# Order of the small products, weights for twelve expert pairs ahead, and when the other pairs' weights are asked for, in a five-stage transformer kernel

## The reference

```
x = x + attention(norm(x))          # 16 heads of 16, rotary embedding, softmax over 512 keys
x = x + moe(norm(x))                # 64 experts, 8 per token, 128 rows at most per expert
x = x + forget_attention(norm(x))   # linear attention with a decay per head and step, biases
x = x + moe(norm(x))                # same weights as the first
```

```
probs = softmax(x @ router_w.T); topk_w, topk_ids = top_k(probs, 8); topk_w /= sum(topk_w)
# each expert e takes its first 128 rows:
h = silu(xb @ w_gate[e]) * (xb @ w_up[e])      # 256 -> 192
y = h @ w_down[e]                              # 192 -> 256, scaled by topk_w, added to its rows
out = sum over the 8 experts of a token + silu(x @ sg) * (x @ su) @ ws_down   # shared expert
```

## Time and profile before

| | us |
|---|---|
| median of 3 runs | 2755.16 (2754.28 to 2756.10) |
| the profiled execution, its time | 2756.48 |
| its span, first to last instruction | 2754.8 |
| attention_project, 0 to 258 | 258 |
| attention_mix, 258 to 1152 | 894 |
| moe_front, moe_experts (first) | 260, 273 |
| forget_attention, 1685 to 2222 | 537 |
| moe_front, moe_experts (second) | 257, 276 |

### The profile page before, as it was taken

How to read it: one execution, slowest core, us unless ns; L and a number is a source line. 1 busy time by engine, 2 the same in 40 slices (tenths; PEclk the granted TensorE clock), 3 DMA queues, 4 the chain that set the end, 5 groups by cost and what they waited for, 6 DMA issues and landing times. The chain is left out here.

```text
span 2754.8 us, 47087 instructions
## 1 busy us (share of the span) xinstructions
PE 2424.5 (88%) x14506; PEld 1327.5 (48%) x14506; DVE 1737.0 (63%) x3661; ACT 1272.0 (46%) x2564; POOL 1128.4 (41%) x1350
## 2 busy tenths in 40 slices
PE   8996899999999999699878883899999979888885
PEld 5653233323333333366456662566666556556663
DVE  7996887788778877288422222688888669632221
ACT  3452576676666667444223220545545424322221
POOL 6888000100000010133136663677777723226664
PEclk9997799999999999899989995999999989999997
DMA  5554323232232321255439982011111036537985
GB/s 165 189 190 160 103 91 95 83 92 84 89 92 88 97 81 47 72 164 195 146 102 247 233 194 54 16 36 36 36 38 30 21 120 202 177 101 193 236 224 104
DMA packets 289374, 325.30 MB, mean 118 GB/s; under 512 B 28944, under 2 KB 270752, under 8 KB 289184
## 3 DMA queue, kind: packets, MB, share of 16 engines
q1 hardware_dynamic: 257536, 274.49, 32.4%
q0 software_dynamic: 27136, 46.16, 8.3%
q10 hardware_dynamic: 4512, 2.40, 0.3%
HBM read 217.23 MB, written 105.19 MB: 117 GB/s over the span
## 5 line engine op out<-in xcount | busy, mean ns | idle before, releaser
L672 DVE TENSOR_REDUCE a_row_max<-a_ps_m 128x2 f32<-128x1024 f32 x512 | 615.0, 1220 | 126.5 <-PE a_ps_m L570 124.4
L720 ACT ACTIVATE a_probs<-a_ps_s 128x512 f32<-128x512 f32 x1024 | 545.7, 600 | 293.7 <-PE a_ps_s L596 293.4
L596 PE MATMUL a_ps_s<-a_qs,a_ks 98*128 98x512 bf16 (+1 forms) x1024 | 319.1, 390 | 9.8 <-ACT a_probs L720 7.5
L611 PE MATMUL a_ps_o<-a_probs,a_va 128*32 128x512 f32 x2048 | 272.3, 604 | 0.8 <-ACT a_o_sb L729 0.8
L1511 POOL TENSOR_TENSOR b_spread<-b_decay,held_own_sb 128x512 f32<-128x512 f32 x256 | 269.1, 1084 | 8.6 <-DVE b_weight L1609 8.6
L570 PE MATMUL a_ps_m<-a_ks,a_qs 48*128 48x512 bf16 x1024 | 207.1, 401 | 45.6 <-DVE a_row_max L672 40.0
L570 PEld LDWEIGHTS a_ps_m<-a_ks,a_qs 48*128 48x128 bf16 x1024 | 49.3, 93 | 342.0 <-DVE a_row_max L672 169.4
L545 POOL DMA_DIRECT2D x<-a_xo x32 | 23.5, 735 | 442.6 <-DVE a_xo L705 442.6
L1609 DVE TENSOR_TENSOR b_weight<-b_ps_s,b_spread 128x512 f32<-128x512 f32 x256 | 163.6, 681 | 17.9 <-PE b_ps_s L1744 17.9
L596 PEld LDWEIGHTS a_ps_s<-a_qs,a_ks 98*128 98x128 bf16 (+1 forms) x1024 | 69.8, 97 | 157.5 <-ACT a_probs L720 86.2
L516 POOL CAST a_high<-a_row_max 128x32 bf16<-128x32 f32 x32 | 6.7, 209 | 321.2 <-DVE a_row_max L672 321.2
(11 more groups left out here) (326 smaller groups left out, 5097.5 us busy)
## 6 DMA issues: line engine op xcount, KB each, us to landing
parts<-a_parts SPq DMA_DIRECT2D x16, 1536.0 KB, 6.2
a_qs<-parts SPq DMA_DIRECT2D x384, 64.0 KB, 2.2
a_ks<-parts SPq DMA_DIRECT2D x384, 64.0 KB, 2.2
m_w_gu<-in_L_ffn_w_gate_dram SPq DMA_DIRECT2D x64, 384.0 KB, 4.0
m_w_gu<-in_L_ffn_w_up_dram SPq DMA_DIRECT2D x64, 384.0 KB, 5.4
m_w_d<-in_L_ffn_w_down_dram SPq DMA_DIRECT2D x64, 384.0 KB, 6.7
rows<-m1f_row SPq DMA_DIRECT2D x16, 640.0 KB, 3.1
rows<-m2f_row SPq DMA_DIRECT2D x16, 640.0 KB, 3.1
```

What stands on the lines that cost most here:

```text
L596: nc.tensor.matmul(s_bank(name, step)[:], ks[u][0:K_ALL[e], h, t * P:(t + 1) * P], qs[u][0:K_ALL[e], h, :], start=True, stop=True).then_in ...
L611: last = nc.tensor.matmul(ps_o[VW * j:VW * (j + 1), :], va[n.u][:, t, (h0 + j) * VW:(h0 + j + 1) * VW], probs[:, group % 2, j, t, :], star ...
L672: nc.vector.tensor_reduce(row_max[:, n.k // 4 % 2, t, :, n.p % 4], m_bank(name, step)[:], AX.X, ALU.max).then_inc(m_drained, 1)
L720: nc.scalar.activation(probs[:, group % 2, j, t, :], s_bank(name, step)[:], ACT.Exp, scale=DK ** -0.5).then_inc(s_drained, 1)
```

## The change

- **attention_mix:** in the lists of PE and DVE and in M_ORDER, the turn of the output moves to behind the second score product, ahead of the values' product; the turn of the maxima to behind it. Both stood between the second and the third of the products for row maxima, and now stand between the first and the second.
- **Expert weights:** there are twelve buffers. Four are memory of their own, four ("early") are the memory that the routing part of `moe_front` uses for x, row and the gates, and four ("kept") that of x_turned. `moe_front` loads twelve pairs: four at steps 16 to 19, four at steps 20 to 23 after the routing part has ended, and four at steps 19, 21, 24 and 26 after the last shared round that lies in their memory. It waits for all twelve at its end. `kept_at` lays the rounds in x_turned so that this works.
- **moe_experts:** the remaining 20 pairs' weights wait for y0 as before, and for a new semaphore `landed`, which POOL raises when its wait for the scatter before has ended. Pair i (12 to 31) waits for the count i - 12 + (i - 12) * 7 // 20 + 1, so 20 requests are spread over 26 scatters. DVE does `compare` and `set_aside` first in a step.
- **forget_attention:** `project_features` is split in `first_features` and `last_features`, with `sum_logs` and `turn_att` between them; ACT does `decays` before `copy_att`.

```diff
@@ -331,7 +332,7 @@
         return at
 
     M_RING, S_RING = 2, 3
-    M_ORDER = [("max0", 0, 1, 0), ("max1", 0, 1, 0), ("shift", L_TURN, 4, 3), ("output", L_OTURN, 2, 1), ("max2", 0, 1, 0), ("max3", 0, 1, 0),
+    M_ORDER = [("max0", 0, 1, 0), ("output", L_OTURN, 2, 1), ("shift", L_TURN, 4, 3), ("max1", 0, 1, 0), ("max2", 0, 1, 0), ("max3", 0, 1, 0),
                ("out0", L_OUT[0], PAIRS, PAIRS - 1), ("out1", L_OUT[1], PAIRS, PAIRS - 1)]
     S_ORDER = [(f"score{i}", L_S, 1, 0) for i in range(8)] + [(f"att{q}", L_ATT[q], PAIRS, PAIRS - 1) for q in range(2)]
     M_AT, S_AT = turns_in_order(M_ORDER, TOTAL + 16), turns_in_order(S_ORDER, TOTAL + 16)
@@ -651,9 +652,8 @@
                     last.then_inc(m_filled, 1)
                 return stage
 
-            walk_pairs(pe, [(0, max_products(0)), (L_S, scores(0)), (L_S, scores(1)), (L_MIX + 1, mix_values(1)),
-                            (0, max_products(1)), (L_S, scores(2)), (L_S, scores(3)), (L_TURN, turn_shift), (L_OTURN, turn_output),
-                            (0, max_products(2)), (L_S, scores(4)), (L_S, scores(5)), (L_MIX, mix_values(0)),
+            walk_pairs(pe, [(0, max_products(0)), (L_S, scores(0)), (L_S, scores(1)), (L_OTURN, turn_output), (L_MIX + 1, mix_values(1)),
+                            (L_TURN, turn_shift), (0, max_products(1)), (L_S, scores(2)), (L_S, scores(3)), (0, max_products(2)), (L_S, scores(4)), (L_S, scores(5)), (L_MIX, mix_values(0)),
                             (0, max_products(3)), (L_S, scores(6)), (L_S, scores(7)),
                             (L_ATT[0], turn_att(0)), (L_ATT[1], turn_att(1)), (L_OUT[0], project(0)), (L_OUT[1], project(1))])
 
@@ -705,7 +705,7 @@
                     nc.vector.tensor_tensor(xo[:, q], out, xr[n.u][:, 2 * q:2 * q + 2, :], ALU.add).then_inc(m_drained, 1)
                 return stage
 
-            walk_pairs(dve, [(0, maxima(0)), (0, maxima(1)), (L_TURN, copy_shift), (L_OTURN, normalise), (0, maxima(2)), (0, maxima(3)),
+            walk_pairs(dve, [(0, maxima(0)), (L_OTURN, normalise), (L_TURN, copy_shift), (0, maxima(1)), (0, maxima(2)), (0, maxima(3)),
                              (L_OUT[0], residual(0)), (L_OUT[1], residual(1))], unrolled=2)
 
...
@@ -871,13 +885,28 @@
                 for to, source in pair_of_weights(const, i, i):
                     sp.dma_start(to, source).then_inc(w_loaded, 16)
 
-            in_turn([(lambda i: i, lambda i: load(i + XB - 1), ROUNDS - XB + 1), (lambda i: ROUNDS + 2 * i, load_weights, HELD),
+            def load_early(i):
+                if i == 0:
+                    sp.wait_ge(gate_done, ROUNDS)
+                    sp.wait_ge(x_was_turned, 2 * ROUNDS)
+                    for k in range(RB):
+                        sp.wait_ge(row_stored[k], 16 * ROUNDS // RB)
+                load_weights(OWN + i)
+
+            def last_round(i):
+
+                return 6 + -(-(i + 1) * XT // KEPT_BUFFERS) - 1
+
+            def load_kept(i):
+                sp.wait_ge(gated, 3 * (last_round(i) + 1))
+                load_weights(OWN + EARLY_BUFFERS + i)
+
+            in_turn([(lambda i: i, lambda i: load(i + XB - 1), ROUNDS - XB + 1), (lambda i: ROUNDS + i, load_weights, OWN),
+                     (lambda i: ROUNDS + L_GATE + 1 + i, load_early, EARLY_BUFFERS), (lambda i: shared_at(last_round(i)) + 1, load_kept, KEPT_BUFFERS),
                      (shared_at, load_residual, ROUNDS),
                      (lambda i: i + L_GATE, store_rows, ROUNDS), (lambda r: shared_at(r) + 1, store, ROUNDS)])
             sp.wait_ge(pad_stored, 16)
-            sp.wait_ge(w_loaded, 48 * HELD)
-            for k in range(RB):
-                sp.wait_ge(row_stored[k], 16 * ROUNDS // RB)
+            sp.wait_ge(w_loaded, 48 * (OWN + EARLY_BUFFERS + KEPT_BUFFERS))
             for k in range(2):
                 sp.wait_ge(stored[k], 16 * ROUNDS // 2)
 
@@ -1022,8 +1051,7 @@
                 def stage(s):
                     act.wait_ge(x_was_turned, 2 * s + q + 1)
                     wait(act, gated, 3 * (s - XT + 1))
-                    first = (TPR * (s % XT) + 2 * q) * P
-                    nc.scalar.activation(x_turned[:, :, first:first + 2 * P], ps_x[:], ACT.Copy).then_inc(x_kept, 1)
+                    nc.scalar.activation(x_turned[:, kept_at(s), :, 2 * q * P:2 * (q + 1) * P], ps_x[:], ACT.Copy).then_inc(x_kept, 1)
                 return stage
 
...
     PAIRS, C = E // 2, 2
     FH = F // C
-    WB, XB, YB, DB = 4, 8, 4, 6
-    LEAD = 2
+    WB, XB, YB, DB = len(const["w_buffers"]), 8, 4, 6
     slots, slots_f = const["slots"], const["slots_f"]
 
...
@@ -1218,7 +1245,7 @@
             for i in range(WB, PAIRS):
                 k = i % WB
                 sp.wait_ge(y0_ready, i - WB + 1)
-                sp.wait_ge(x_turned, i - LEAD + 1)
+                sp.wait_ge(landed, i - WB + (i - WB) * 7 // (PAIRS - WB) + 1)
                 for to, source in pair_of_weights(const, i, k):
                     sp.dma_start(to, source).then_inc(w_loaded[k], 16)
 
@@ -1236,6 +1263,7 @@
                 pool.wait_ge(y1_done, i + 1)
                 pool.wait_ge(y0_done, i + 1)
                 wait(pool, scattered, 32 * i)
+                passed_by(pool, landed)
 
                 for j, index in ((1, slots_1[:, i:i + 1]), (0, slots[:, 2 * i:2 * i + 1])):
...
@@ -1352,7 +1380,7 @@
                 wait(dve, scattered, 32 * (i - YB + 1))
                 nc.vector.tensor_copy(y[:, i % YB, 0, :], ps_y[i % 2][:, 0, :]).then_inc(y0_done, 1)
 
-            in_turn([(L_GU, hidden(0)), (L_DOWN, copy_first), (L_GU, hidden(1)), (L_SAME, compare), (L_SAME, set_aside)])
+            in_turn([(L_SAME, compare), (L_SAME, set_aside), (L_GU, hidden(0)), (L_DOWN, copy_first), (L_GU, hidden(1))])
 
 
 def forget_attention(nc, x_in, x_out, const):
@@ -1683,8 +1711,8 @@
                 wait(act, out_ready, n - 1)
                 nc.scalar.activation(attT[:, n % 2], ps_w[:, 0:2, :], ACT.Copy).then_inc(attT_done, 1)
 
-            in_turn([(L_VF, evacuate_values), (L_PV, copy_output), (L_TURN, evacuate_x), (L_LOGS, gate_exponentials), (L_OUT, copy_att),
-                     (L_UPTO, decays), (L_FEED, exponentials)])
+            in_turn([(L_VF, evacuate_values), (L_PV, copy_output), (L_TURN, evacuate_x), (L_LOGS, gate_exponentials), (L_UPTO, decays),
+                     (L_OUT, copy_att), (L_FEED, exponentials)])
 
         @block.tensor
         def _(pe):
@@ -1726,13 +1754,15 @@
                 wait(pe, decay_done, n)
                 nc.tensor.matmul(ps_a[:, 0:D], later[:], log_upto[:, n % 2].rearrange("p h t -> p (h t)"), start=True, stop=True).then_inc(sums_ready, 1)
 
-            def project_features(n):
+            def first_features(n):
                 sg, blk = n // SG, n % SG
                 pe.wait_ge(xnT_done, SG * (sg + 1))
                 wait(pe, phi_done, n)
-                for c in range(2):
-                    last = nc.tensor.matmul(ps_p[:], w_qk[:, c, blk * P:(blk + 1) * P], xnT[:, sg % 2, c, :], start=c == 0, stop=c == 1)
-                last.then_inc(p_ready, 1)
+                nc.tensor.matmul(ps_p[:], w_qk[:, 0, blk * P:(blk + 1) * P], xnT[:, sg % 2, 0, :], start=True, stop=False)
+
+            def last_features(n):
+                sg, blk = n // SG, n % SG
+                nc.tensor.matmul(ps_p[:], w_qk[:, 1, blk * P:(blk + 1) * P], xnT[:, sg % 2, 1, :], start=False, stop=True).then_inc(p_ready, 1)
 
             def scores(n):
                 sg, g = n // SG, n % SG
@@ -1775,8 +1805,8 @@
                     last = nc.tensor.matmul(out, attT[:, n % 2, c, :], w_o[:, c, :], start=False, stop=c == 1)
                 last.then_inc(out_ready, 1)
 
-            in_turn([(L_VF, project_values), (L_S, scores), (L_PV, mix_values), (L_TURN, turn_x), (L_OUT, turn_output), (L_FEED, project_features),
-                     (L_OUT, turn_att), (L_UPTO, sum_logs), (L_OUT, project_out)])
+            in_turn([(L_VF, project_values), (L_S, scores), (L_PV, mix_values), (L_TURN, turn_x), (L_OUT, turn_output), (L_FEED, first_features),
+                     (L_UPTO, sum_logs), (L_OUT, turn_att), (L_FEED, last_features), (L_OUT, project_out)])
 
 
...
@@ -1846,8 +1878,17 @@
 
     def mixture(tag, x_in, x_out):
         with (nc.sbuf_tensor(tag + "_slots", [P, E], u32) as slots, nc.sbuf_tensor(tag + "_slots_f", [P, E], fp32) as slots_f,
-              nc.sbuf_tensor(tag + "_w_gu", [P, PAIRS_HELD, 2, 2, 2, F], fp32) as w_gu, nc.sbuf_tensor(tag + "_w_d", [F // 2, PAIRS_HELD, 2, 2, D], fp32) as w_d):
-            const = dict(held, slots=slots, slots_f=slots_f, w_gu=w_gu, w_d=w_d, w_gate=a["L0_ffn_w_gate"], w_up=a["L0_ffn_w_up"], w_down=a["L0_ffn_w_down"])
+              nc.sbuf_tensor(tag + "_own", [P, OWN * (GU + WD)], fp32) as own, nc.sbuf_tensor(tag + "_early", [P, EARLY * (GU + WD)], fp32) as early,
+              nc.sbuf_tensor(tag + "_kept", [P, KEPT * (GU + WD)], fp32) as kept):
+
+
+            buffers = []
```

(6 more changed lines are left out.)

53 lines of the change are left out of this document (33 added, 20 removed).

## The result

| | before | after |
|---|---|---|
| median, us | 2754.72 | 2707.82 |
| range of the runs, us | 2751.31 to 2756.10 | 2707.73 to 2711.89 |
| span of the profiled execution, us | 2754.8 | 2705.8 |

The ratio of the two is 0.9839, 95% interval 0.9823 to 0.9855: some 44 us are gained (47 by the medians), where 85 were forecast. The time lies in the range for 8 in 10 (2638 to 2712), near its upper end, and outside the forecast's own range of 2650 to 2695.

The account below looks back on a forecast made before the run. Expert stages were taken as bound by a scatter chain stretched by weight transfers, the two attention stages by PE. From 2756.48 us, -42 - 30 - 13 + 0 = -85 gave 2671.5, median 2670; own range 2650 to 2695, 8 in 10 2638 to 2712.

Parts of the forecast that it names:

- rival 3: attention_mix and forget_attention: the PE edits only move their waits, DVE holding the next product or step; 2714 us, chance 0.08.
- the period of a loaded scatter: Expert stages: distance between pairs' first scatters with a weight request, taken as 7.4 us; 219 against 238.6, -20 per stage.
- rival 1: Expert stages: a request at the scatter's start doubles its transfers, 6.5 + 2.35 = 8.85 us per loaded period; 2729, chance 0.14.
- The ceiling of 9.62 to 10.12: Expert stages: upper limit in us for a loaded period, from profiled distances with a request just behind the scatter's start.
- Unloaded and last distances: Expert stages: scatter distances without a weight request, 6 at 6.5 us, and the last 5 at 6.37 us.
- The bound that was named, 0.41 of issue time: Expert stages: POOL raising the new semaphore costs between 0 and 0.41 us per scatter; 0.05 taken, +1 per stage.
- Compare first: Expert stages: compare ahead in DVE's list takes 0.70 us off each PE step, seen only in the filling; -2 per stage.
- moe_front: Both fronts: loading eight more pairs, 9.4 MB, is hidden by PE's work; 0, between -2 and +8 us per stage.
- attention_mix: Moved turns of output and maxima end PE's 0.35 us waits: 96 x 0.35 = 34, less 3; -30, between 0 and -37.
- forget_attention: Splitting the features removes PE's 0.2 us wait per step for the copy of att; 64 steps, -13, between 0 and -16.
- the signs named: Expert distances 7.0 to 7.1 us, DMA share below 0.96, no compare wait; maxima wait under 8; fronts within 3 us.
- rival 4: Expert stages: the scatters run at the floor, 6.5 us each, -38 - 1 per stage; 2636 us, chance 0.12.

Follow-up runs that it names:

- after_again: The kernel after, unchanged, run on the second chip beside later kernels; 2709.15 us, ratio to before 0.9850.
- by_products: The kernel after without the wait for `landed`: twelve buffers kept, weights asked for as soon as PE has made y0 of pair i - 12; ratio to before 0.9838.
- behind_scatters: The kernel after with `landed` raised behind the issue of a pair's two scatters instead of ahead of them; 2753.59 us, ratio to before 0.9957.
- compare_last: The kernel after with DVE's compare and set-aside put back behind the hidden rows; 2711.46 us, ratio to before 0.9880.
- spread_direct: The kernel after without `landed`: SP waits for the scatters' own landings, each pair's three weight transfers asked for apart, 60 over 26 scatters; 2680.83 us, ratio to before 0.9757.
- no_later_weights: The kernel after with weights of expert pairs 12 to 31 never loaded in both expert stages, `landed` still raised; ratio to before 0.9678.

## Why the prediction was right in sign and off in size

The median, 2707.8, is nearer to rival 3's 2714 than to the forecast's 2670. That is a coincidence of sums: rival 3 had the two edits of PE's order gain nothing, and they gained 15 and 11 us, while the expert stages, which it left at -42, gave -22.

1. *Expert stages, the period of a loaded scatter: 7.4 was taken, 7.76 and 8.10 measured.* This is the term that was mis-sized, worth 7 and 14 us. The sum took it near the transfer time of its bytes, 7.2 us. That time was nearly reached where two loaded distances followed each other (7.31 at 238 GB/s), but the average has what the unloaded one leaves behind (8.16 and 8.70 for the six behind one), and the next scatter waits for the landing of the one before, not for the bytes. In after_again the second scatter of a pair lands 5.1 and 5.2 us behind its start in a loaded distance, 3.9 and 3.8 in an unloaded one; rival 1 had 2.35 us more. The reason given, that one request per scatter would not pile up, was not what counted: by_products has no such tie and the same time. Rival 1's size is what a request just behind a scatter's start costs (behind_scatters, 8.84 and 8.79 for its 8.85). In after the request leaves one microsecond before that place, since `landed` is raised ahead of the scatter, and after lies between the forecast and rival 1. Why a microsecond of start saves as much as it does was not shown packet by packet. The ceiling of 9.62 to 10.12 was read from distances that hold two requests each, six transfers by SP's timeline, so it was no ceiling for one request.
2. *Unloaded and last distances*: 6.72 and 6.5 for 6.5 and 6.37, because of the semaphore on POOL. It was charged 0.05 us at each scatter and costs 0.13, 4 us a stage in place of 1 (and 0.13 of each loaded distance above is the same). The kernel without it is 11.5 us faster than after_again, 3 to 4 of which stay open. The bound that was named, 0.41 of issue time, held it; the value chosen was too low.
3. *Compare first*: -2 per stage forecast, -2.7 and -2.1 by compare_last, hidden everywhere else as said.
4. *moe_front*: 0 forecast, -1 and 0 measured. Eight more pairs fit beside PE's work: the DMA share rose from 0.49 to 0.62 in the first, and PE's busy time stayed (229 and 228 us).
5. *attention_mix*: -30 forecast, -15 measured. The mechanism was right and the price was not: the recorded wait of 0.35 went, but only 0.25 of it is saved per turned output (64 x 0.25 = 16, and 14.1 measured), and the 32 turned maxima gave 4 us, not the 8 that were charged (32 x 0.35 less 3). The held the 0.35; that a turn stands 0.1 us later behind its scores in the new place was in no row, and the step's length before and after would have been the safer unit. The rest is at the stage's ends: 17.6 us between the first and last reduction, 15 for the stage. PE's wait for the maxima is 11.5 and not under 8; it stayed below the 25 of rival 3.
6. *forget_attention*: -13 forecast, -11 measured, 0.20 us a step as worked out. It is PE's order that does it.

Of the signs named, the DMA share in the experts' middle fell (0.79 and 0.77 over the first 26 distances; before it is 0.92 over the same 26, the 0.96 being a stretch of 47 us), PE's wait for the compare went (0.5 us once in after_again), both fronts kept their length; the mean distance is 7.35 and 7.58 us and not 7.0 to 7.1, and no loaded distance mean is above the 8.5 of rival 1.

Rival 4 had all scatters at the floor, 201 us. Of the kernels that load all weights spread_direct is the nearest, with 217. With no later weights at all, but with the semaphore, 207 and 208 are left (no_later_weights).

## What to carry to other kernels

When small transfers that wait for each other share the DMA engines with large ones, read how long the chain is with and without the large ones, and then spread these: an even two or three at each link took 17 us off a kernel that asked for three or none (2697.64 to 2680.83). A wait in a profile is worth the change in the step's length, not its own length. And a semaphore that is raised on the engine that sets the pace is part of the chain (0.13 us each time here); let the waiting engine look at the event itself. To find what a chain waits for, take the time from the supposed release to the next start over many steps: where it is the same to a few nanoseconds, that is the release, whatever the brackets of single rows name.

## What the runs showed that was not expected

- The request that waits for a semaphore raised behind two indirect DMAs in POOL's program left SP 0.33 us after the first of them began, while POOL worked on them for 3.5 us (behind_scatters).
- From a scatter's landing to the next scatter's start took 0.79 us in the median in the first expert stage, and 0.92 with one semaphore raised between, in loaded and unloaded distances alike.
- Asking for 1.18 MB one microsecond later, just behind a scatter's start in place of just ahead of it, made each such distance 0.6 to 1.1 us longer, some 30 us for the kernel (2753.59, with by_products at 2723.86 beside it).
- Scatters and gathers keep the sixteen DMA engines busy half of the time at 89 GB/s; weights bring it to 0.9 at 238.
- From the first gather to the first scatter of an expert stage took 28 to 30 us in the first group of runs and 21 to 24 in all others, with the same instructions.
